# Sparse feed-forward with features on the partitions, for pairs of blocks of rows

## The chip, the cores and the metric

The kernel runs on one core of a Trainium2 chip. The metric is the device time of one execution in microseconds (us), taken as the median over runs. The whole kernel is a chain of eight layers (four pairs of attention and feed-forward); the change touches one of them, the second.

## The reference, cut to what matters

The state `x` has 16 blocks of 128 rows with 256 features. The stage that is changed computes `x = x + ffn(layernorm(x))`, all in float32, with weights 256x1024, 256x1024 and 1024x256:

```
def _sparsify_2to4(h):
    g = h.reshape(B, S, I // 4, 4)
    a = jnp.abs(g)
    _, idx = jax.lax.top_k(a, 2)
    pos = jnp.arange(4)
    mask = (pos == idx[..., 0:1]) | (pos == idx[..., 1:2])
    return (g * mask.astype(g.dtype)).reshape(B, S, I)
h = silu(einsum('bsh,hi->bsi', x, w_gate)) * einsum('bsh,hi->bsi', x, w_up)
h_sparse = _sparsify_2to4(h)
return einsum('bsi,ih->bsh', h_sparse, w_down)
```

Of every four neighbouring features of the 1024, the two of larger size are kept and the others set to zero.

## The kernel before

`sparse_ffn` works on one block `t` (128 rows) at a time. Rows lie on the partitions. `norm_row` (ScalarE) normalises a block into `xn`; `turn_row` (TensorE) transposes its two 128x128 halves into the bank `row_t`; `move_row` (ScalarE) copies them to `xt`. `gate_up` multiplies with `xt` as the stationary operand and 512 columns of weights as the moving one, for two halves `n` of the 1024 features: the rows stay on the partitions of the banks `gate[n]` and `up[n]`, and the features run along them. A float32 matmul of the program stands in the trace as two matmul instructions, each with a weight load of its own; a transpose is one.

Then, for each half: `silu` (ScalarE) reads `gate`, `multiply` (VectorE) forms `h` from it and `up`, `sizes` (ScalarE) takes the absolute value. `sparsify` (VectorE) compares the four features of each group pairwise. As the four are neighbours in a row, every operand of these comparisons and of the four products that write `kept` steps over four elements, 16 bytes. The comparisons give 0 or 1 in 16-bit numbers (`near`, `far`, `ends`, `mids`), which are added and compared with a count.

`turn_down` then transposes `kept` in eight 128x128 pieces into the banks `turned`, ScalarE copies them to `ht` in two pieces (`move`), and eight matmuls of the program with 256 moving columns, over the eight pieces, sum up `down`. `update` (VectorE) adds that to `x` and takes the statistics of the next norm.

The order of each engine is written by hand, with semaphores between engines. TensorE: `gate_up(t)`, `turn_row(t + 1)`, `turn_down(t - 1)`. VectorE: `multiply(t)`, `sparsify(t)`, `update(t - 1)`. Blocks 1 to 14 run in a hardware loop (`Fori`) on each of the three engines; blocks 0 and 15 are written out. At the end `turn_ahead` transposes the first rows of the next stage. The weights were loaded during the stage before. GpSimd only takes two roots, and no transfer but instructions runs beside the stage.

Of the kernel before, what the change touches and what calls it, by code (L numbers as in the profile page):

```python
# [5 lines left out]
BF16 = mybir.dt.bfloat16  # L6
# [3 lines left out]
ALU = mybir.AluOpType  # L10
# [4 lines left out]
P = 128  # L15
# [598 lines left out]
def sparse_ffn(nc, mem, norm, norm_next):  # L614

    I = 1024
    N2 = I // 2
    Q = I // 4
    ctx = Stage(nc)
    with ctx:  # L620
# [6 lines left out]
        def signal(what, per=1, credit=0):  # L627
            return Signal(ctx, nc, f"sf_{what}", per, credit)

        w = mem.sf  # L630
        xt = sb("xt", [P, HC, P])
        act_g = sb("act_g", [P, I])
        h, size = sb("h", [P, I]), sb("size", [P, I])
        kept = sb("kept", [P, I])

        near = sb("near", [P, 2, Q], BF16)
        far = sb("far", [P, 2, Q], BF16)
        ends, mids = sb("ends", [P, Q], BF16), sb("mids", [P, Q], BF16)
        outer, inner = sb("outer", [P, 2, Q], BF16), sb("inner", [P, 2, Q], BF16)
        outer_n, inner_n = sb("outer_n", [P, 2, Q], BF16), sb("inner_n", [P, 2, Q], BF16)  # L640
# [4 lines left out]
        down, row_t = bank("down"), bank("row_t")  # L645
        xn, ahead = sb("xn", [P, H]), sb("ahead", [P, GROUP, H])
        row_normed, row_turned, row_moved = signal("row_normed"), signal("row_turned"), signal("row_moved")
        ahead_normed, ahead_turned, ahead_moved = signal("ahead_normed"), signal("ahead_turned"), signal("ahead_moved")
        gated = signal("gated", 2, 1)
        silued = signal("silued", 2, 2)  # L650
        multiplied = signal("multiplied", 2, 2)
        sized = signal("sized", 2)
        compared = signal("compared", 4)
        counted = signal("counted", 5)
        sparse = signal("sparse", 1, 1)
        turn = signal("turn", 2, 2)
        moved = signal("moved", 2, 2)
        downed = signal("downed", 1, 1)
        added = signal("added", 1, 1)
        stat = signal("stat")  # L660

        with nc.Block() as block:
# [6 lines left out]
            def _(pe):  # L669
                for s, n in ((gated, 1), (turn, 2), (downed, 1)):  # L670
                    pe.sem_inc(s.sem, n)
                pe.wait_ge(mem.sf_loaded.sem, 16 * mem.sf_loads)

                def turn_row(t):
                    pe.wait_ge(row_normed.sem, row_normed.at(t))
                    for c in range(HC):
                        last = pe.transpose(row_t[:, c * P:(c + 1) * P], xn[:, c * P:(c + 1) * P], mem.ident[:, :])
                    last.then_inc(row_turned.sem, 1)
# [8 lines left out]
                def gate_up(t):  # L687
                    pe.wait_ge(row_moved.sem, row_moved.at(t))
                    for n in range(2):
                        pe.wait_ge(silued.sem, silued.at(t, n - 2))  # L690
                        pe.wait_ge(multiplied.sem, multiplied.at(t, n - 2))
                        for out, weight in ((gate, w.wg), (up, w.wu)):
                            for c in range(HC):
                                last = pe.matmul(out[n][:, :], xt[:, c, :], weight[:, c, n * N2:(n + 1) * N2], start=(c == 0), stop=(c == HC - 1))
                        last.then_inc(gated.sem, 1)

                def turn_down(t):
                    pe.wait_ge(sparse.sem, sparse.at(t))
                    for n in range(2):
                        pe.wait_ge(moved.sem, moved.at(t, n - 2))  # L700
                        for k in range(4):
                            c = 4 * n + k
                            last = pe.transpose(turned[n][:, k * P:(k + 1) * P], kept[:, c * P:(c + 1) * P], mem.ident[:, :])
                        last.then_inc(turn.sem, 1)
                    pe.wait_ge(added.sem, added.at(t, -1))
                    for n in range(2):
                        pe.wait_ge(moved.sem, moved.at(t, n))
                        for c in range(4 * n, 4 * n + 4):
                            last = pe.matmul(down[:, 0:H], ht[:, c, :], w.wd[:, c, :], start=(c == 0), stop=(c == I // P - 1))
                    last.then_inc(downed.sem, 1)  # L710

                turn_row(0)
                gate_up(0)
                turn_row(1)
                with pe.Fori(1, B - 1) as t:
                    gate_up(t)
                    turn_row(t + 1)
                    turn_down(t - 1)
                gate_up(B - 1)
                turn_down(B - 2)  # L720
                turn_ahead(0, row_t)
                pe.wait_ge(silued.sem, silued.at(B - 1, 0))
                turn_ahead(1, gate[0])
                turn_down(B - 1)

            @block.scalar
            def _(act):
                act.sem_inc(silued.sem, 2)
                act.sem_inc(moved.sem, 2)

                def silu(t, n):
                    act.wait_ge(gated.sem, gated.at(t, n))
                    act.wait_ge(multiplied.sem, multiplied.at(t, n - 2))
                    act.activation(act_g[:, n * N2:(n + 1) * N2], gate[n][:, :], ACT.Silu).then_inc(silued.sem, 1)

                def sizes(t, n):
                    act.wait_ge(multiplied.sem, multiplied.at(t, n))
                    if n == 0:
                        act.wait_ge(sparse.sem, sparse.at(t, -1))
                    act.activation(size[:, n * N2:(n + 1) * N2], h[:, n * N2:(n + 1) * N2], ACT.Abs).then_inc(sized.sem, 1)  # L740

                def move(t):
                    act.wait_ge(downed.sem, downed.at(t, -1))
                    for n in range(2):
                        act.wait_ge(turn.sem, turn.at(t, n))
                        act.activation(ht[:, 4 * n:4 * n + 4, :].rearrange("p c s -> p (c s)"), turned[n][:, :], ACT.Copy).then_inc(moved.sem, 1)

                def norm_row(t):
                    if not isinstance(t, int) or t >= 1:
                        act.wait_ge(row_turned.sem, row_turned.at(t - 1))  # L750
                    act.activation(xn[:, :], mem.x_tile(t), ACT.Identity, bias=norm.shift[:, bass.ds(t, 1)],
                                   scale=norm.rstd[:, bass.ds(t, 1)]).then_inc(row_normed.sem, 1)

                def move_row(t):
                    act.wait_ge(row_turned.sem, row_turned.at(t))
                    act.activation(xt[:, :, :].rearrange("p c s -> p (c s)"), row_t[:, 0:H], ACT.Copy).then_inc(row_moved.sem, 1)
# [12 lines left out]
                norm_row(0)  # L769
                move_row(0)  # L770
                norm_row(1)
                silu(0, 0)
                sizes(0, 0)
                silu(0, 1)
                sizes(0, 1)
                move_row(1)
                act.wait_ge(norm.shifted.sem, norm.shifted.at(GROUPS - 1))
                with act.Fori(1, B - 1) as t:
                    norm_row(t + 1)
                    silu(t, 0)  # L780
                    sizes(t, 0)
                    silu(t, 1)
                    move(t - 1)
                    sizes(t, 1)
                    move_row(t + 1)
                silu(B - 1, 0)
                sizes(B - 1, 0)
                silu(B - 1, 1)
                move(B - 2)
                sizes(B - 1, 1)  # L790
                for t in range(GROUP):
                    norm_ahead(t)
                move_ahead(0, row_t)
                move_ahead(1, gate[0])
                move(B - 1)

            @block.vector
            def _(dve):
                dve.sem_inc(multiplied.sem, 2)
                dve.sem_inc(sparse.sem, 1)  # L800
                dve.sem_inc(added.sem, 1)
                groups = size[:, :].rearrange("p (q u v) -> p v u q", u=2, v=2)
                fours = size[:, :].rearrange("p (q f) -> p f q", f=4)
                h4, kept4 = (x[:, :].rearrange("p (q f) -> p f q", f=4) for x in (h, kept))

                def multiply(t):
                    dve.wait_ge(sparse.sem, sparse.at(t, -1))
                    for n in range(2):
                        dve.wait_ge(silued.sem, silued.at(t, n))
                        dve.tensor_tensor(h[:, n * N2:(n + 1) * N2], act_g[:, n * N2:(n + 1) * N2], up[n][:, :], ALU.mult).then_inc(multiplied.sem, 1)  # L810

                def sparsify(t):
                    dve.wait_ge(sized.sem, sized.at(t, 1))
                    dve.tensor_tensor(near[:, :, :], groups[:, 0], groups[:, 1], ALU.is_ge).then_inc(compared.sem, 1)
                    dve.tensor_tensor(far[:, 0, :], fours[:, 1], fours[:, 3], ALU.is_ge)
# [3275 lines left out]
```

## Time and profile before

| | |
|---|---|
| time, median of 3 runs | 2070.43 us (2069.07 to 2079.79) |
| profiled execution | span 2074.5 us; its own time is not given beside the span |
| granted TensorE clock, mean over the span | 0.960 of full speed |
| this stage, first gate matmul to last statistics | 491.7 to 693.7 us |
| TensorE busy, 530 to 650 us | 117.51 of 120 us |
| VectorE busy, same stretch | 89.69 of 120 us |
| ScalarE busy, same stretch | 41.86 of 120 us |

Starts are in us from the span's start. In the timeline several instructions of one kind are merged into a row with their count; the time beside it runs from the first one's start to the last one's end. PE is the matmul side of TensorE and PEld its weight loads, which run beside the matmuls; DVE is VectorE, ACT ScalarE, POOL GpSimd. The ends of matmuls are modelled, so their spacing is read from starts.

### The profile page before, as it was taken

What the parts mean: (1) busy time and instruction counts of PE and PEld (TensorE: products, weight loads), DVE (VectorE), ACT (ScalarE), POOL (GpSimd) and SP (SyncE); (2) the same over time, 40 slices, a digit from 0 to 9 for tenths busy, and PEclk for the clock granted to TensorE, in tenths of its full rate; (3) what the DMA queues carried; (4) which work ended last, traced back from release to release, by engine and by line L of the source; (5) the groups of instructions that cost most, each with busy time, mean ns of one, the idle gap of its engine ahead of it and who ended that gap; (6) DMA issues with size and microseconds to landing.
All of it is one profiled execution on the core that took longest, in us unless ns stands there. A gap on an engine that the chain in (4) does not pass through costs nothing. (4 is left out here: it accounts for less than half of the span.)

```text
span 2074.5 us, 42486 instructions
## 1 busy us (share of the span) xinstructions
PE 1853.4 (89%) x12207; PEld 1251.6 (60%) x12216; DVE 1266.8 (61%) x4137; ACT 1026.9 (50%) x2698; POOL 730.7 (35%) x707
## 2 busy tenths in 40 slices
PE   7999999998999888878999989969978799999755
PEld 4677777775565566545666766735545557777533
DVE  6666666665777344656343334368979545656698
ACT  5555555553333443312444434348879524444586
POOL 3333333331000202566455555533300106676410
PEclk9999999999999898979999999989999898999998
DMA  8990000000000000253777776510010111211100
GB/s 305 283 274 1 0 0 0 0 1 0 0 0 0 1 1 33 76 197 120 170 162 169 169 155 136 92 59 2 2 64 1 64 43 26 42 39 36 43 18 24
DMA packets 145607, 145.55 MB, mean 70 GB/s; under 512 B 49376, under 2 KB 133568, under 8 KB 145344
## 3 DMA queue, kind: packets, MB, share of 16 engines
q1 hardware_dynamic: 122432, 113.81, 19.5%
q0 software_dynamic: 23040, 30.01, 8.2%
q8 instruction: 75, 1.23, 0.2%
q14 instruction: 60, 0.49, 0.1%
HBM read 137.12 MB, written 66.44 MB: 98 GB/s over the span
## 5 line engine op out<-in xcount | busy, mean ns | idle before, releaser
L1709 POOL DMA_INDIRECT expert_sums<-moe_rows_in,moe_to x128 | 198.2, 1549 | 158.7 <-DMA expert_sums<-moe_rows_in,moe_to 91.9
L1782 PE MATMUL moe_gate<-moe_places,moe_xt 128*128 x512 | 175.3, 465 | 3.4 <-issue 1.9
L3329 DVE CUSTOM_DVE_ANT_0 ctxt<-wa_score,early 128x128 f32<-128x128 f32 x512 | 114.2, 286 | 101.3 <-PE wa_score L3179 101.3
L1975 DVE COPY moe_ht_e<-moe_turned 128x256 f32<-128x256 f32 x128 | 54.4, 425 | 193.9 <-PE moe_turned L1790 192.5
L570 ACT ACTIVATE ga_prob<-ga_score,ga_neg_max 128x128 f32<-128x128 f32 x256 | 99.6, 390 | 125.7 <-DVE ga_neg_max L443 125.7
L3141 POOL TENSOR_TENSOR ctxt<-ctxt,wa_top 128x512 f32<-128x512 f32 x128 | 131.6, 1040 | 75.4 <-DVE wa_top L3329 75.4
L2065 POOL TENSOR_TENSOR ln_rstd<-ln_var,half 128x4 f32<-128x4 f32 (+1 forms) x16 | 21.5, 1346 | 362.1 <-DVE ln_var L2061 362.1
L190 POOL TENSOR_TENSOR ga_q_inv<-ga_q_sum,half 128x4 f32<-128x4 f32 x64 | 64.4, 1007 | 224.3 <-DVE ga_q_sum L426 224.3
L3278 ACT ACTIVATE wa_pt<-wa_turned 128x512 f32<-128x512 f32 x128 | 76.5, 598 | 129.7 <-PE wa_turned L3188 129.7
L325 PE MATMUL ga_summed<-ga_wo,ga_out_t 128*128 128x256 f32 x512 | 121.2, 380 | 0.7 <-ACT ga_out_t L578 0.7
L1782 PEld LDWEIGHTS moe_gate<-moe_places,moe_xt 128*128 128x128 f32 x512 | 90.5, 189 | 47.2 <-issue 12.1
L249 PE MATMUL ga_proj<-early,ga_xt 128*128 128x512 f32 x252 | 118.6, 593 | 0.0
L1116 POOL DMA_INDIRECT slot_x<-early x96 | 97.8, 1019 | 56.4 <-issue 27.4
L439 DVE SCALAR_TENSOR_TENSOR ga_score<-ga_scored,ga_q_inv,ga_mask 128x128 f32<-128x128 f32 x256 | 72.2, 344 | 51.6 <-PE ga_scored L297 50.1
L325 PEld LDWEIGHTS ga_summed<-ga_wo,ga_out_t 128*128 128x128 f32 x512 | 92.3, 190 | 11.0 <-ACT ga_out_t L578 1.1
L1889 ACT ACTIVATE moe_act_e<-moe_gate 128x176 f32<-128x176 f32 x128 | 40.6, 317 | 100.0 <-PE moe_gate L1782 99.3
L3179 PE MATMUL wa_score<-wa_keys,wa_qd 32*128 32x128 f32 x1024 | 78.9, 294 | 11.6 <-DVE wa_top L3329 9.0
L3188 PE MATMUL wa_turned<-ident,ctxt 128*128 128x128 f32 x512 | 84.3, 290 | 0.0
L3179 PEld LDWEIGHTS wa_score<-wa_keys,wa_qd 32*128 32x128 f32 x1024 | 66.6, 197 | 26.6 <-issue 23.2
L431 DVE COPY ga_qt<-ga_turned 128x512 f32<-128x512 f32 x63 | 43.5, 690 | 62.5 <-PE ga_turned L289 62.4
L297 PEld LDWEIGHTS ga_scored<-ga_kt,ga_qt 128*128 128x128 f32 x512 | 63.3, 191 | 23.6 <-DVE ga_qt L431 13.9
L556 ACT ACTIVATE ga_square<-ga_q_tok 128x128 f32<-128x128 f32 x256 | 75.0, 294 | 1.3 <-DVE ga_q_tok L394 1.3
(491 smaller groups left out, 4777.6 us busy)
## 6 DMA issues: line engine op xcount, KB each, us to landing
moe_places<-in_L_ffn_packed SPq DMA_DIRECT2D x128, 608.0 KB
slot_x<-zeros SPq DMA_DIRECT2D x24, 1076.0 KB, 16.3
moe_rows_in<-slot_x SPq DMA_DIRECT2D x128, 134.5 KB, 3.0
wa_v<-v_ctx SPq DMA_DIRECT2D x16, 180.0 KB, 3.1
early<-in_L_xattn_Wq SPq DMA_DIRECT2D x5, 512.0 KB, 7.8
x<-in_x SPq DMA_DIRECT2D x4, 512.0 KB, 9.6
ga_wo<-in_L_xattn_Wo SPq DMA_DIRECT2D x1, 2048.0 KB, 15.1
expert_sums<-zeros SPq DMA_DIRECT2D x2, 1024.0 KB, 8.4
```

The lines of the kernel that those rows point to most:

```text
L249: last = pe.matmul(proj[m % 2][:, :], lhs[:, c, :], weight[:, c, :], start=(c == 0), stop=(c == HC - 1))
L325: last = pe.matmul(summed[:, 0:H], out_t[:, h, :], w.wo[:, h, :], start=(h == 0), stop=(h == NH - 1))
L556: last = act.activation(square[:, h, :], q_tok[:, n % 2, h * D:(h + 1) * D], ACT.Square, accum_out=q_sum[:, n % 2, h:h + 1])
L570: last = act.activation(prob[:, n % 2, part], score[:, n % 2, part], ACT.Exp, bias=neg_max[:, n % 2, h:h + 1], accum_out=total[:, n % 2, h ...
L1116: pool.indirect_dma_start(out=self.mem.slot_x, out_offset=bass.IndirectOffsetOnAxis(ap=self.slot_to[:, t, k:k + 1], axis=0), in_=self.mem. ...
L1709: pool.indirect_dma_start(out=mem.sums[j % SUMS], out_offset=bass.IndirectOffsetOnAxis(ap=to[:, j:j + 1], axis=0), in_=y[:, j, :], in_offs ...
L1782: last = pe.matmul(both[j % 2][:, 0:2 * FE], xt[:, j % 2, c, :], packed[:, place, c * 2 * FE:(c + 1) * 2 * FE].rearrange("p a n -> p (a n) ...
L3141: pool.tensor_tensor(unit, unit, top[:, k % LOWS, :].unsqueeze(2).to_broadcast([P, QUAD, P]), ALU.subtract).then_inc(lowered.sem, 1)
L3179: last = pe.matmul(score[(QUAD * u + r) % 3][:, x * P:(x + 1) * P], w.qd[rows, j % 2, QUAD * u + x, :], w.keys[rows, j % 2, QUAD * u + x, ...
L3188: last = pe.transpose(turned[k % 2][:, x * P:(x + 1) * P], low[:, k % LOWS, x, :], mem.ident[:, :])
L3278: act.activation(pt[:, (k // 2) % 2, :, k % 2, :], turned[k % 2][:, :].rearrange("p (x m) -> p x m", x=QUAD), ACT.Exp).then_inc(pt_moved.s ...
L3329: ins = dve.tensor_tensor_reduce(unit[:, x, :], score[k % 3][:, x * P:(x + 1) * P], w.table[:, k, x, :], 1.0, NEVER, ALU.add, ALU.max, top ...
```

## The change

The stage is computed with features on the partitions, for a pair `p` of blocks (256 rows) at a time. The columns of the gate and up weights are reordered on the host (and the rows of the down weights with them), so that the four features of a group lie in four different 128-column slices, at the same place in each. There are two sets `s` of four slices. `gate_up(p, u)` takes two slices (a unit `u`, four to a pair): the weights' 128x128 pieces are now the stationary operand, and the 256 normalised rows the moving one. `h`, `size` and `kept` are laid out as slice by row, so each comparison and each product of `sparsify(p, s)` reads and writes whole runs of 256 elements. One of the comparisons is now one instruction of 512 in place of two of 256.

`kept` then has features on the partitions already. `go_down(p, s)` uses it as the stationary operand directly: the transposes into `turned`, the copies to `ht` and the banks for them are gone. `down` has two banks, one for each block of the pair; `xt` and `kept` have two buffers.

The order is new, and there is no hardware loop: all eight pairs are written out on every engine.

```
 def host_layout(inputs):
+    for name in ("L0_ffn_w_gate", "L0_ffn_w_up"):
+        a[name] = np.ascontiguousarray(a[name].reshape(H, 2, P, 4).transpose(0, 1, 3, 2).reshape(H, 1024))
+    a["L0_ffn_w_down"] = np.ascontiguousarray(a["L0_ffn_w_down"].reshape(2, P, 4, H).transpose(0, 2, 1, 3).reshape(1024, H))
...
-        xt = sb("xt", [P, HC, P])
-        h, size = sb("h", [P, I]), sb("size", [P, I])
-        kept = sb("kept", [P, I])
-        ht = sb("ht", [P, I // P, P])
-        turned = [bank(f"turned{j}") for j in range(2)]
+        xt = sb("xt", [P, 2, HC, N])
+        act_g = sb("act_g", [P, 2, 2, N])
+        h, size = sb("h", [P, SETS, V, N]), sb("size", [P, SETS, V, N])
+        kept = sb("kept", [P, 2, SETS * V, N])
+        down, row_t = [bank(f"down{j}") for j in range(2)], bank("row_t")
...
             def _(pe):
+                def turn_rows(p):
+                    pe.wait_ge(row_normed.sem, row_normed.at(2 * p + 1))
+                    behind(pe, row_moved, p - 1)
+                    for c in range(HC):
+                        for i in range(2):
+                            last = pe.transpose(row_t[:, (2 * c + i) * P:(2 * c + i + 1) * P], xn[:, i, c * P:(c + 1) * P], mem.ident[:, :])
...
+                def gate_up(p, u):
+                    n = p * UNITS + u
+                    if u == 0:
+                        pe.wait_ge(row_moved.sem, row_moved.at(p))
+                    behind(pe, multiplied, n - 2)
+                    for out, weight in ((gate, w.wg), (up, w.wu)):
+                        for v in range(2):
+                            f = 2 * u + v
                             for c in range(HC):
-                                last = pe.matmul(out[n][:, :], xt[:, c, :], weight[:, c, n * N2:(n + 1) * N2], start=(c == 0), stop=(c == HC - 1))
+                                last = pe.matmul(out[n % 2][:, v * N:(v + 1) * N], weight[:, c, f * P:(f + 1) * P], xt[:, p % 2, c, :], start=(c == 0), stop=(c == HC - 1))
+                    last.then_inc(gated.sem, 1)
+
+                def go_down(p, s):
+                    pe.wait_ge(sparse.sem, sparse.at(SETS * p + s))
+                    for i in range(2):
+                        if s == 0:
+                            behind(pe, added, 2 * (p - 1) + i)
+                        for f in range(V * s, V * (s + 1)):
+                            last = pe.matmul(down[i][:, 0:H], kept[:, p % 2, f, i * P:(i + 1) * P], w.wd[:, f, :], start=(f == 0), stop=(f == V * SETS - 1))
+                        if s == SETS - 1:
+                            last.then_inc(downed.sem, 1)
...
+                turn_rows(0)
+                for p in range(PAIRS):
+                    gate_up(p, 0)
+                    gate_up(p, 1)
+                    if p >= 1:
+                        go_down(p - 1, 0)
+                        go_down(p - 1, 1)
+                    if p + 1 < PAIRS:
+                        turn_rows(p + 1)
+                    gate_up(p, 2)
+                    gate_up(p, 3)
                 turn_ahead(0, row_t)
+                go_down(PAIRS - 1, 0)
+                pe.wait_ge(silued.sem, silued.at(PAIRS * UNITS - 2))
                 turn_ahead(1, gate[0])
+                go_down(PAIRS - 1, 1)
...
             def _(act):
+                norm_rows(0)
+                move_rows(0)
+                for p in range(PAIRS):
+                    silu(p, 0)
+                    sizes(p, 0)
+                    if p + 1 < PAIRS:
...
+                        norm_rows(p + 1)
+                    silu(p, 1)
+                    sizes(p, 1)
...
+                    silu(p, 2)
+                    sizes(p, 2)
+                    if p + 1 < PAIRS:
+                        move_rows(p + 1)
+                    silu(p, 3)
+                    sizes(p, 3)
...
             def _(dve):
+                def sparsify(p, s):
+                    q = SETS * p + s
+                    of, value = size[:, s, :, :], h[:, s, :, :]
+                    every = size[:, s, :, :].rearrange("p (u v) n -> p v u n", v=2)
+                    out = kept[:, p % 2, V * s:V * (s + 1), :]
+                    dve.wait_ge(sized.sem, sized.at(p * UNITS + 2 * s + 1))
+                    dve.tensor_tensor(near[:, :, :], every[:, 0], every[:, 1], ALU.is_ge).then_inc(compared.sem, 1)
+                    dve.tensor_tensor(far[:, :, :], of[:, 0:2], of[:, 2:4], ALU.is_ge).then_inc(compared.sem, 1)
+                    dve.tensor_tensor(ends[:, :], of[:, 0], of[:, 3], ALU.is_ge).then_inc(compared.sem, 1)
+                    dve.tensor_tensor(mids[:, :], of[:, 1], of[:, 2], ALU.is_ge).then_inc(compared.sem, 1)
...
+                    dve.tensor_tensor(outer[:, :, :], near[:, :, :], far[:, :, :], ALU.add).then_inc(counted.sem, 1)
                     for k in range(2):
+                        dve.tensor_tensor(inner[:, k, :], far[:, 1 - k, :], near[:, k, :], ALU.subtract).then_inc(counted.sem, 1)
...
+                    dve.scalar_tensor_tensor(out[:, 0], outer_n[:, 0, :], 2.0, value[:, 0], ALU.is_ge, ALU.mult)
...
+                for p in range(PAIRS):
+                    multiply(p, 0)
+                    if p == PAIRS - 1:
+                        dve.wait_ge(stat.sem, stat.at(B - GROUP - 1))
+                        norm_next.variance(dve, 0, B - GROUP)
+                    multiply(p, 1)
+                    if p == PAIRS - 1:
+                        norm_next.shifts(dve, 0, 0, B - GROUP)
+                    sparsify(p, 0)
+                    if p >= 1:
+                        update(2 * p - 2)
+                        update(2 * p - 1)
+                    multiply(p, 2)
+                    multiply(p, 3)
+                    sparsify(p, 1)
                 update(B - 2)
                 update(B - 1)
```

On ScalarE `silu(p, u)` and `multiply(p, u)` handle 512 elements as before, `norm_rows(p)` two blocks, and `move_rows(p)` one copy of 512.

## Rows read from the trace of the kernel before

**Rows 1.** Head of the page: span, busy time and instructions by engine.
```profile
span 2074.5 us, 42486 instructions
PE 1853.4 (89%) x12207; PEld 1251.6 (60%) x12216; DVE 1266.8 (61%) x4137; ACT 1026.9 (50%) x2698; POOL 730.7 (35%) x707
```

**Rows 2.** Windows: PE, PEld, DVE, ACT, POOL busy, granted clock, DMA share, GB/s.
```profile
1450.00:1500.00 50.00, 50.00 (x450) 28.94 (x442) 45.54 (x107) 42.31 (x108) 19.34 (x21) 1.00 0.01 2
530.00:650.00 120.00, 117.51 (x423) 71.83 (x422) 89.69 (x182) 41.86 (x80) 0.00 (x0) 1.00 0.00 0
```

**Rows 3.** Waits, 491.5 to 692 us: who for whom, total us, times, longest.
```profile
ACT sf_act_g L734 <- PE sf_up L694: 94.0, 30, 6.0
...
DVE sf_near L814 <- ACT sf_size L740: 14.8, 16, 1.0
...
PE sf_down L709 <- ACT sf_ht L746: 4.3, 15, 0.6
```

**Rows 4.** Timeline of one turn of the loop: start, us, engine, line.
```profile
602.60 0.60 ACT L734 ACTIVATE sf_act_g<-sf_gate 128x512 f32<-128x512 f32 x1 [5.55 <-PE sf_up L694]
...
605.87 0.91 PEld L703 LDWEIGHTS sf_turned<-ident,sf_kept 128*128 128x128 f32 x8
...
607.26 3.32 PEld L709 LDWEIGHTS sf_down<-sf_wd,sf_ht 128*128 128x128 f32 x16 [0.49 <-ACT sf_ht L746]
...
608.25 1.10 DVE L814 TENSOR_TENSOR sf_near<-sf_size 128x512 bf16<-128x512 f32 x1 [0.97 <-ACT sf_size L740]
608.37 0.61 ACT L751 ACTIVATE sf_xn<-x,ln_shift,ln_rstd 128x256 f32 x1
609.25 0.62 DVE L815 TENSOR_TENSOR sf_far<-sf_size 128x256 bf16<-128x256 f32 x1
609.78 0.62 DVE L816 TENSOR_TENSOR sf_far<-sf_size 128x256 bf16<-128x256 f32 x1
...
610.61 0.41 PEld L694 LDWEIGHTS sf_gate<-sf_wg,sf_xt 128*128 128x128 f32 x2
...
611.25 0.19 PEld L694 LDWEIGHTS sf_gate<-sf_wg,sf_xt 128*128 128x128 f32 x1 [0.24 <-issue]
...
611.68 0.19 PEld L694 LDWEIGHTS sf_gate<-sf_wg,sf_xt 128*128 128x128 f32 x1 [0.24 <-issue]
...
614.38 0.66 DVE L839 SCALAR_TENSOR_TENSOR sf_kept<-sf_outer_n,sf_h 128x256 f32<-128x256 bf16 x1
...
614.53 0.60 ACT L734 ACTIVATE sf_act_g<-sf_gate 128x512 f32<-128x512 f32 x1 [5.56 <-PE sf_up L694]
...
614.91 0.45 DVE L844 TENSOR_TENSOR x<-x,sf_down 128x256 f32 x1
...
616.00 0.69 DVE L810 TENSOR_TENSOR sf_h<-sf_act_g,sf_up 128x512 f32<-128x512 f32 x1
```

**Rows 5.** Groups by form, whole span: count, busy us, mean ns, idle before.
```profile
L420 DVE TENSOR_TENSOR ga_k_rms<-ga_k_tok,ga_k_inv 128x512 f32<-128x512 f32 x16 | 11.1, 692 | 7.9 <-POOL ga_k_inv L185 7.9
...
L823 DVE TENSOR_TENSOR sf_outer<-sf_near,sf_far 128x256 bf16<-128x256 bf16 x32 | 7.9, 294 | 0.0
...
L826 DVE TENSOR_TENSOR sf_inner_n<-sf_inner,sf_mids 128x512 bf16<-128x512 bf16 x16 | 6.8, 427 | 0.0
...
L1474 DVE TENSOR_TENSOR la_mixed_t<-la_wide,la_z_inv 128x256 f32<-128x256 f32 x16 | 6.8, 425 | 1.5
...
L1098 DVE SCALAR_TENSOR_TENSOR early<-early 128x128 f32<-128x128 f32 x3 | 0.9, 291 | 0.1
```

**Rows 6.** Timeline of the stage's start: the first matmuls after a pause.
```profile
491.70 3.68 PE L694 MATMUL sf_gate<-sf_wg,sf_xt 128*128 128x512 f32 x4 [0.47 <-ACT sf_xt L756]
```

**Rows 7.** Timeline of the stage's end: last transposes, last matmuls, last statistics.
```profile
686.51 1.97 PE L703 MATMUL sf_turned<-ident,sf_kept 128*128 128x128 f32 x8 [3.13 <-DVE sf_kept L839]
...
688.46 4.35 PE L709 MATMUL sf_down<-sf_wd,sf_ht 128*128 128x256 f32 x16
...
693.30 0.43 DVE L846 BATCH_NORM_STATS2 stats<-x 128x6 f32<-128x256 f32 x1
```

More of the change, by code:

```diff
@@ L642, in sparse_ffn @@
+        near, far = sb("near", [P, 2, N], BF16), sb("far", [P, 2, N], BF16)
+        ends, mids = sb("ends", [P, N], BF16), sb("mids", [P, N], BF16)
+        outer, inner = sb("outer", [P, 2, N], BF16), sb("inner", [P, 2, N], BF16)
+        outer_n, inner_n = sb("outer_n", [P, 2, N], BF16), sb("inner_n", [P, 2, N], BF16)
         gate = [bank(f"gate{j}") for j in range(2)]
         up = [bank(f"up{j}") for j in range(2)]
-        turned = [bank(f"turned{j}") for j in range(2)]
-        down, row_t = bank("down"), bank("row_t")
@@ L662, in sparse_ffn, with behind @@
+        downed, added, stat = signal("downed"), signal("added"), signal("stat")
+        def behind(engine, sig, n):
+            if n >= 0:
+                engine.wait_ge(sig.sem, sig.at(n))
         with nc.Block() as block:
@@ L697, in turn_down @@
[L697 to L710, printed above, removed]
@@ L736, in sizes @@
[L736 to L746, printed above, removed]
@@ L748, in norm_row, with silu @@
[L748 to L756, printed above, removed]
+                def silu(p, u):
+                    n = p * UNITS + u
+                    act.wait_ge(gated.sem, gated.at(n))
+                    behind(act, multiplied, n - 2)
+                    act.activation(act_g[:, n % 2, :, :].rearrange("p v n -> p (v n)"), gate[n % 2][:, :], ACT.Silu).then_inc(silued.sem, 1)
@@ new lines, in sizes, with norm_rows @@
+                def sizes(p, u):
+                    s, k = divmod(u, 2)
+                    act.wait_ge(multiplied.sem, multiplied.at(p * UNITS + u))
+                    if k == 0:
+                        behind(act, sparse, SETS * (p - 1) + s)
+                    act.activation(size[:, s, 2 * k:2 * k + 2, :], h[:, s, 2 * k:2 * k + 2, :], ACT.Abs).then_inc(sized.sem, 1)
+                def norm_rows(p):
+                    behind(act, row_turned, p - 1)
+                    for i in range(2):
+                        t = 2 * p + i
+                        act.activation(xn[:, i, :], mem.x[:, t, :], ACT.Identity, bias=norm.shift[:, t:t + 1],
+                                       scale=norm.rstd[:, t:t + 1]).then_inc(row_normed.sem, 1)
@@ L758, in norm_ahead, with move_rows @@
+                def move_rows(p):
+                    act.wait_ge(row_turned.sem, row_turned.at(p))
+                    if p >= 2:
+                        act.wait_ge(gated.sem, gated.at((p - 2) * UNITS + UNITS - 1))
+                    act.activation(xt[:, p % 2, :, :].rearrange("p c n -> p (c n)"), row_t[:, :], ACT.Copy).then_inc(row_moved.sem, 1)
                 def norm_ahead(t):
@@ L768, in _ @@
                 act.wait_ge(norm.shifted.sem, norm.shifted.at(GROUPS - 2))
[L769 to L792, printed above, removed]
+                norm_rows(0)
[4 more added lines that the diff above has]
+                    if p + 1 < PAIRS:
+                        if 2 * (p + 1) == B - GROUP:
+                            act.wait_ge(norm.shifted.sem, norm.shifted.at(GROUPS - 1))
+                        norm_rows(p + 1)
+                    silu(p, 1)
+                    sizes(p, 1)
+                    if p == PAIRS - 1:
+                        for t in range(GROUP):
+                            norm_ahead(t)
+                    silu(p, 2)
[4 more added lines that the diff above has]
+                    sizes(p, 3)
```

132 lines of the change are left out of this document (34 added, 98 removed).

## The prediction

> **What bounds the kernel now.** I read the page's head first: TensorE is busy 89% of a span of 2074.5 us [rows 1], so a stage is bound by it unless its own rows say otherwise. Then the windows of this stage: from 530 to 650 us TensorE is busy 117.51 of 120 us at a granted clock of 1.00 (2.4 GHz), VectorE 89.69 and ScalarE 41.86 [rows 2]. The waits say the same from the other side: ScalarE's first `silu` of a block waits for the up matmuls, 94.0 us in all, while TensorE waits only 4.3 us in 15 waits, for the copies to `ht` [rows 3]. So TensorE's own work sets the pace, with one short stall in each block.
>
> The timeline gives the period: `silu` starts at 602.60 and again at 614.53, so a block takes 11.93 us and a pair 23.86 [rows 4]. Inside it, wide gate loads follow each other every 0.43 us (611.25, 611.68): that is the pace of 512 moving columns. Sixteen make 6.86 us. The eight transposes of `kept` take 0.91 us, so 0.114 each, and the two row transposes 0.23. Then 0.49 us of stall for `ht`, and 16 down matmuls of 256 columns from 607.26 to the next gate load at 610.61, 3.35 us or 0.209 each. These sum to 11.84 of the 11.93; the loop's edge shows no gap of its own.
>
> **The change on TensorE.** A unit is 16 matmul instructions of 256 columns. Half of 0.43 is 0.215, and the down matmuls show 0.209 for the same form (128x128 stationary, 256 moving, float32); I take 0.213. A pair then has 64 in `gate_up` (13.63 us, a unit being 3.41), 32 in `go_down` (6.82) and 4 row transposes (0.46): 20.9 us against 23.86. The columns streamed are the same; what goes is two times 0.91 of transposes and 0.49 of stall with the small gaps beside it. With 0.209 and 0.215 a pair is 20.5 or 21.1, so the gain is 2.8 to 3.4 us a pair; I take 3.0.
>
> **Whether the narrow matmuls hide their loads.** A load takes 0.19 us [rows 4] and now stands before every 0.213 us of gate and up streaming, in place of every 0.43. In the down matmuls of before it does too, and they still come every 0.209: the load is hidden, with only 0.02 us to spare. The Trainium skill (TensorE: Matmul & The Clock Gate, under "The mechanism") says otherwise: a weight load overlaps with matmuls in flight only if it goes to other row groups, and all these loads fill all rows. By that rule, with the rows' durations, a pair of before would take 38.6 us and one of after 39.7, some 9 us slower in all. The trace does not agree, since a pair of before takes 23.86.
>
> **VectorE.** The set of `sparsify` has the same elements as a block had, 1024 a partition, so there is one set for each block as before. From `near` at 608.25 to the end of the last `kept` at 615.04 it takes 6.8 us [rows 4]. Instructions overlap by some 0.09 us (`far` lasts 0.62, the next starts 0.53 on). No row shows a contiguous compare; the bounds are the strided price (512 in 1.10, 256 in 0.62 to 0.66) and contiguous float32 rows of the same kind: 512 in 0.692 and 256 in 0.425 [rows 5]. I take the contiguous end, since 0.692 has both inputs in SBUF as here and differs from `near` only in its stride. For the products that write `kept`, an instruction with a scalar over 128 columns takes 0.291, so 0.42 for 256. Start to start: `near` and `far` 0.60 each, `ends` and `mids` 0.335 each, `outer` 0.335 (0.427 for 512 in 16 bit), `inner` twice 0.20 (0.294), the two sums 0.335 each, `kept` four times 0.335. That is 4.6, and 4.7 to the end of the last: 2.1 less than 6.8.
>
> **Does that leave TensorE the bound?** The new order makes a ring between VectorE and ScalarE, since `multiply(p, 2)` stands behind both updates and a set, and `silu(p, 1)` behind `sizes(p, 0)` and `norm_rows`. From the end of one pair's second set: multiply 0.69, sizes 0.63, two norms 1.0 (0.61 each less the overlap), silu 0.60, multiply 0.69, sizes 0.63, the first set 4.7, two updates 2.2 (614.91 to 616.00 is one), multiply 0.69, sizes 0.63, `move_rows` 0.60, silu 0.60, multiply 0.69, sizes 0.63, the second set 4.7: 19.7 us. Twelve handovers add 0.6 at 0.05 each, an estimate (at nothing the ring is 19.4, at 0.12 each it draws level with TensorE), and ScalarE's overlaps give back 0.3. So 20.0 us against TensorE's 20.9: TensorE stays the bound by 0.9 us a pair. The ring binds once a set takes more than 5.15 us, and each 0.1 us beyond costs 0.2 a pair. `go_down(p-1, 1)` needs a set that ends about 7 us into the pair and comes at 10.2; `move_rows` ends about 0.9 us before the next pair's first matmul. What ScalarE loses (the copies to `ht`) was beside the path and counts only as that stall. GpSimd and the queues carry no new work.
>
> **Start and end.** Before, the first gate matmul starts at 491.70 and four of them take 3.68 us [rows 6], a pace of about 0.85, the lower level of the clock (1.2 GHz). This costs 1.7 us over some 3.4, and will again. The first pair must norm two blocks (0.5 more), turn four pieces (0.2) and copy 512 instead of 256 (0.2): start at 492.6. In pair 0 the second half's inputs come late: unit 0 ends at 497.7; silu, multiply, sizes, two norms, silu, multiply and sizes follow by 503.0, the set ends at 507.7, `multiply(0, 2)`, sizes and `move_rows(1)` at 509.7, while unit 3 ends at 508.4: a stall of 1.4 once. Then TensorE: 492.6 + 32 units 109.1 + 1.7 + seven times 6.82 (47.7) + seven times 0.46 (3.2) + 1.4 = 655.7. The last set needs silu, multiply and sizes (2.3 with handovers) and 4.7: 662.7. Here TensorE has stood idle and pays the low clock again, as before (686.51: eight transposes in 1.97, sixteen matmuls in 4.35 [rows 7]). `go_down(7, 1)` has 16 matmuls: 3.4 + 1.6 + 0.3 = 5.3 us, then add and statistics 1.1: 669.1. Before, the stage ends at 693.73 [rows 7]. The sum is -24.6 us; I take -24. Against the profiled span that is 2050.5. The profiled span lies 4 us above the median, and the same difference against the median of 2070.43 gives 2046.4.
>
> **Written out.** The three engines lose their loops. That brings more code, at about 4.8 matmuls a us. In stretches that are written out TensorE issued 450 in 50 us, 9 a us, and was busy all of it [rows 2], so I cost it at nothing; if code came late it would show as gaps at each pair.
>
> **Rivals.**
> 1. *The ring binds a little* (0.08). The `kept` products keep their strided pace, 0.54 start to start, for their mix of 16- and 32-bit operands. A set is 5.5, the ring 21.6, 0.7 above TensorE in seven pairs, and 1.6 more at the end: 24 less 6.5 gives 17.5, so 2053. For it: no row has that mix contiguous. Against: the whole strided price is explained by the step.
> 2. *The price does not depend on the step* (0.06). Sets stay 6.8; the ring is 24.2 against 23.86 now, so 2 us more over seven pairs, less a little for the shorter tail: 2072, no change. For it: both operands read SBUF. Against: 0.692 against 1.10 for 512.
> 3. *The loads show* (0.04), the other side. If the gate and up loads are not hidden, 64 times 0.19 is 12.2 us a pair, 97 in all, less 24: 2143. The gain of 3.0 us a pair is gone from 0.047 us exposed for each of 64. For it: only 0.02 us of room. Against: the down matmuls' own pace.
> 4. *Anything unnamed* (0.02), about no change, late code or a semaphore chain that I missed.
>
> **How the numbers follow.** The forecast has 0.80. A measurement of this kernel can tell about 0.5%, 10.4 us. Forecast and rival 1 lie beyond it: faster 0.88. Rivals 2 and 4 give 0.08 of same, rival 3 0.04 of slower. The gain a pair of 2.8 to 3.4 gives 22 to 28 us; with the set's bounds 17 us at the low end, and the spread of the runs themselves, the range is 2038 to 2058. It leaves out rivals 2 to 4, and a tenth of the rest.
>
> **What the profile would show.** No rows for `turned` and `ht`. Gate and up matmuls of 256 columns every 0.21 us. `near` and `far` at 0.69 for 512, `ends`, `mids` and `kept` at 0.42. Pairs of 20.9 us, TensorE hardly waiting; the stage's last statistics at 669 or so. The forecast is wrong if TensorE waits for `row_moved` (then the ring binds), or if narrow matmuls come slower than every 0.22 us.

## The result, and the profile after

The changed kernel takes 2047.37 us in the median (2043.93 to 2050.54, 4 runs) against 2069.75 (2068.96 to 2079.79, 4 runs) for the kernel before: a ratio of 0.9885 with a 95% interval of [0.9862, 0.9908], so 19 to 29 us less. Timed again on another chip beside later experiments (6 runs against 11), it gave 0.9878 [0.9839, 0.9917]. The forecast was 2046.4, in a range of 2038 to 2058.

First the window that answers to [rows 2]. TensorE now has no idle time in it at all, and VectorE's busy time fell from 89.69 to 76.81 us.

```profile
530.00:650.00 120.00, 120.00 (x568) 105.65 (x567) 76.81 (x195) 36.45 (x64) 2.27 (x1) 1.00 0.00 1
```

The waits of the changed kernel from 491.5 to 668 us, answering to [rows 3] (who for whom: total us, times, longest):

```profile
ACT sf_act_g L729 <- PE sf_up L693: 70.7, 24, 7.3
...
DVE sf_near L801 <- ACT sf_size L736: 10.4, 15, 0.7
...
PE sf_down L702 <- DVE sf_kept L826: 2.5, 1, 2.5
...
PE sf_gate L693 <- ACT sf_xt L749: 2.1, 2, 1.4
```

TensorE's waits are one at the end, for the last set (2.5 us), and those at the start for `xt`, of which 1.4 is the stall in pair 0. None is left in the pairs between; before, there were 15, about one in every block.

The timeline of one pair, weight loads alone, answering to [rows 4]:

```profile
567.41 0.57 PEld L674 LDWEIGHTS sf_row_t<-ident,sf_xn 128*128 128x128 f32 x4
...
571.30 1.70 PEld L693 LDWEIGHTS sf_gate<-sf_xt,sf_wg 128*128 128x128 f32 x8
573.03 1.70 PEld L693 LDWEIGHTS sf_up<-sf_xt,sf_wu 128*128 128x128 f32 x8
574.76 1.70 PEld L693 LDWEIGHTS sf_gate<-sf_xt,sf_wg 128*128 128x128 f32 x8
...
581.66 6.88 PEld L702 LDWEIGHTS sf_down<-sf_wd,sf_kept 128*128 128x128 f32 x32
588.57 0.58 PEld L674 LDWEIGHTS sf_row_t<-ident,sf_xn 128*128 128x128 f32 x4
```

A unit goes from 571.30 to 574.76, 3.46 us, 0.216 a matmul. The down matmuls take 6.91, and the pair, from one turn of the rows to the next, 21.16 us: 2.7 less than the 23.86 of two blocks before. The groups of VectorE, answering to [rows 5] and to the strided rows of [rows 4]:

```profile
L801 DVE TENSOR_TENSOR sf_near<-sf_size 128x512 bf16<-128x512 f32 x16 | 11.1, 692 | 10.4 <-ACT sf_size L736 10.4
L802 DVE TENSOR_TENSOR sf_far<-sf_size 128x512 bf16<-128x512 f32 x16 | 10.9, 684 | 0.0
...
L803 DVE TENSOR_TENSOR sf_ends<-sf_size 128x256 bf16<-128x256 f32 x16 | 6.7, 419 | 0.0
...
L819 DVE SCALAR_TENSOR_TENSOR sf_kept<-sf_outer_n,sf_h 128x256 f32<-128x256 bf16 x16 | 6.7, 417 | 0.1
```

Start and end of the stage, answering to [rows 6] and [rows 7]:

```profile
493.79 3.68 PE L693 MATMUL sf_gate<-sf_xt,sf_wg 128*128 128x256 f32 x8 [0.69 <-ACT sf_xt L749]
...
511.39 1.99 PE L693 MATMUL sf_gate<-sf_xt,sf_wg 128*128 128x256 f32 x8 [1.39 <-ACT sf_xt L749]
```

```profile
666.15 3.72 PE L702 MATMUL sf_down<-sf_wd,sf_kept 128*128 128x256 f32 x16 [2.49 <-DVE sf_kept L826]
...
670.37 0.43 DVE L833 BATCH_NORM_STATS2 stats<-x 128x6 f32<-128x256 f32 x1
```

From the first row norm (491.24, before 490.08) to the last statistics' end (670.80, before 693.73) the stage takes 179.6 us, before 203.6: 24.1 less. The profiled span fell by 32.0, from 2074.5 to 2042.5. The first attention stage was 1.2 longer here, so 9 us fell after this stage, where no code changed, 7.7 of them between the start of the next stage and the first matmuls of the experts, some 280 us later. There the granted clock of the one profile and of the other differ. Before:

```profile
694.40:720.00 25.60, 22.94 (x100) 13.23 (x104) 2.07 (x9) 11.60 (x17) 7.57 (x16) 0.81 0.01 2
...
800.00:830.00 30.00, 28.10 (x240) 22.86 (x237) 13.01 (x39) 11.71 (x23) 14.18 (x15) 0.83 0.16 56
```

After, in the corresponding stretches:

```profile
671.50:697.00 25.50, 22.70 (x136) 13.35 (x136) 4.47 (x12) 12.76 (x20) 8.28 (x17) 1.00 0.01 2
...
777.00:807.00 30.00, 29.11 (x280) 21.91 (x280) 18.51 (x48) 12.94 (x26) 18.18 (x19) 1.00 0.20 70
```

This goes with the clock, not with the change. The stretch takes 275.6 us in this profile, at a mean granted clock of 0.94, and 279.7 in the second profile of the same kernel, at 0.91. The kernel before has 283.3 at 0.90; but its old order written out (below) has 278.5 at 0.93, and the changed order with strided compares (below) 283.0 at 0.90. So the stage is best read by its own pairs, and the medians of many runs for the rest.

### The profile page after: what moved, and what is told of

It is laid out like the page before. It is cut to its first block and busy times, and to the rows that moved or that the text cites. A ratio compares the mean times of both kernels' runs of the same rounds, so it can differ in the third digit from the quotient of the medians.

```text
span 2042.5 us, 42221 instructions
## 1 busy us (share of the span) xinstructions
PE 1822.0 (89%) x12335; PEld 1277.1 (63%) x12344; DVE 1233.2 (60%) x4121; ACT 1011.1 (50%) x2658; POOL 732.3 (36%) x707
```

## The experiments

**Is it the loops?** The kernel before with its loops written out:

```
-                with pe.Fori(1, B - 1) as t:
+                for t in range(1, B - 1):
```

and the same on ScalarE and VectorE.

> The kernel before with its three hardware loops written out, nothing else. Theory T (TensorE's own work sets the pace, the loops cost nothing): the stage from the first row norm to the last statistics stays at 203.6 us within 1 us, a block at 11.93 us, the time within 0.3%. Rival W (part of the gain comes from writing out): the stage falls by 5 us or more.

Ratio to before 0.9992 [0.9966, 1.0018]. In the timeline of ScalarE `move_row` comes every 12.05 us, where before it was 11.93:

```profile
587.43 0.39 ACT L756 ACTIVATE sf_xt<-sf_row_t 128x256 f32<-128x256 f32 x1
...
599.48 0.38 ACT L756 ACTIVATE sf_xt<-sf_row_t 128x256 f32<-128x256 f32 x1
```

Writing out gives nothing; it costs 0.12 us a block. The rows show where: from the first transpose of `kept` to the first down matmul TensorE takes 1.44 us (585.24 to 586.68), before 1.28 (605.98 to 607.26), and its waits for `ht` sum to 6.4 us against 4.3. Why the copies to `ht` come later is open. The stage was 208.1 us, 4.5 more than before, outside what theory T allowed: 1.7 from the blocks, the rest at start and end, where the clock was lower. The granted clock was 0.81 from 488 to 515 us (0.94 in before's profile), and the last sixteen down matmuls took 5.25 us (before 4.35).

**Is it VectorE's contiguous operands?** The kernel before with only its columns reordered:

```
-                groups = size[:, :].rearrange("p (q u v) -> p v u q", u=2, v=2)
-                fours = size[:, :].rearrange("p (q f) -> p f q", f=4)
+                groups = size[:, :].rearrange("p (u v q) -> p v u q", u=2, v=2)
+                fours = size[:, :].rearrange("p (f q) -> p f q", f=4)
...
+    for name in ("L0_ffn_w_gate", "L0_ffn_w_up"):
+        a[name] = np.ascontiguousarray(a[name].reshape(H, 256, 4).transpose(0, 2, 1).reshape(H, 1024))
+    a["L0_ffn_w_down"] = np.ascontiguousarray(a["L0_ffn_w_down"].reshape(256, 4, H).transpose(1, 0, 2).reshape(1024, H))
```

`h4` and `kept4` are regrouped in the same way.

> The kernel before, rows still on the partitions, but with gate and up columns reordered so that the four features of a group lie 256 apart, and all operands of the sparsify set are contiguous. Both theories expect near at 0.69 and kept at 0.42 us, a set shorter by 2.1 us. Theory T: a block stays at 11.93 us, only the last set at the stage's end counts, the stage falls by about 2 us, the time by 2. Rival V (the gain comes from VectorE's cheaper set): the stage falls by 10 us or more, towards the 24 of the change.

Ratio 0.9986 [0.9961, 1.0011]. Its groups, and two copies of the rows in ScalarE's timeline:

```profile
L814 DVE TENSOR_TENSOR sf_near<-sf_size 128x512 bf16<-128x512 f32 x16 | 11.1, 693 | 15.0 <-ACT sf_size L740 15.0
...
L837 DVE SCALAR_TENSOR_TENSOR sf_kept<-sf_outer_n,sf_h 128x256 f32<-128x256 bf16 x16 | 6.7, 419 | 0.0
```

```profile
595.98 0.39 ACT L756 ACTIVATE sf_xt<-sf_row_t 128x256 f32<-128x256 f32 x1
...
607.91 0.39 ACT L756 ACTIVATE sf_xt<-sf_row_t 128x256 f32<-128x256 f32 x1
```

The set is as cheap as in the changed kernel, and the block is still 11.93 us. The stage fell by 3.4 us to 200.2, all at its ends, against 2 expected. The last set is 1.95 us shorter (4.79 for 6.74). Another 1.1 us lies behind it and is the clock's: before's profile has the low level there (transposes 1.97 us, down matmuls 4.35 [rows 7]), this one the high level (1.09 and 3.69). As TensorE sets the pace, VectorE's 2 us a block bought nothing but the tail.

**Does the changed order need the contiguous operands?** The changed kernel, with `size` stored so that the compares are strided again:

```
-        h, size = sb("h", [P, SETS, V, N]), sb("size", [P, SETS, V, N])
+        h, size = sb("h", [P, SETS, V, N]), sb("size", [P, SETS, N, V])
...
-                    act.activation(size[:, s, 2 * k:2 * k + 2, :], h[:, s, 2 * k:2 * k + 2, :], ACT.Abs).then_inc(sized.sem, 1)
+                    act.activation(size[:, s, :, 2 * k:2 * k + 2].rearrange("p n v -> p v n"), h[:, s, 2 * k:2 * k + 2, :], ACT.Abs).then_inc(sized.sem, 1)
```

> The changed kernel with size stored with the four features innermost, so that the four compares are strided again while the rest stays contiguous. A set grows by 1.25 us (near 0.4, far 0.4, ends and mids 0.2 each). Ring theory: the ring of about 20.0 us grows by 2.5 to 22.5 and passes TensorE's 21.2; 1.3 us a pair in seven pairs and 1.3 at the end, 10 to 11 us slower; if the strided writes also lengthen the absolute values on ScalarE beyond 0.63 us, each 0.1 us of that adds 0.4 a pair. Rival (TensorE has ample room, no ring): only the 1.3 us at the end.

Ratio 0.9948 [0.9918, 0.9977] to before, so more than half of the gain is gone. A pair takes 22.9 us, and TensorE waits for `xt`:

```profile
PE sf_gate L693 <- ACT sf_xt L749: 11.9, 7, 3.3
```

```profile
L736 ACT ACTIVATE sf_size<-sf_h 128x512 f32<-128x512 f32 x32 | 36.0, 1124 | 65.4 <-DVE sf_h L793 65.4
L801 DVE TENSOR_TENSOR sf_near<-sf_size 128x512 bf16<-128x512 f32 x16 | 17.4, 1088 | 18.1 <-ACT sf_size L736 18.1
```

The compares are at their strided price, and ScalarE's strided write too (1.124 us, 0.630 contiguous). The stage takes 197.4 us, 17.8 more than the changed kernel's 179.6. The expectation gives 10 to 11, and some 14 more for ScalarE's writes at the price measured; it is too high since the ring is narrower than it says, as the padding below shows. So the reordering is not what gains the time, but the new order can't do without it: in each pair VectorE and ScalarE wait for each other in a ring, and a slow set makes it longer than TensorE's work.

**Does TensorE's work set the pace?** The changed kernel with the transposes put back, unread:

```
                     for i in range(2):
+                        for k in range(V):
+                            pe.transpose(turned[:, k * P:(k + 1) * P], kept[:, p % 2, V * s + k, i * P:(i + 1) * P], mem.ident[:, :])
```

> The changed kernel with the eight transposes of kept for each block put back on TensorE, into a bank that nobody reads; no copies, no wait. Theory T: each costs its 0.114 us on the path, 128 of them 14.6 us, a pair goes from 21.2 to 23.0 us. Rival (the ring of VectorE and ScalarE sets the pace of the changed kernel): less than 7 us, since TensorE would have room.

Ratio 0.995 [0.9929, 0.9971]. The row transposes of two pairs in the timeline of the loads:

```profile
595.61 0.58 PEld L674 LDWEIGHTS sf_row_t<-ident,sf_xn 128*128 128x128 f32 x4
...
618.53 0.57 PEld L674 LDWEIGHTS sf_row_t<-ident,sf_xn 128*128 128x128 f32 x4
```

A pair is 22.92 us, 1.76 more: sixteen times 0.110. In the pairs each transpose stands on the path in full. The stage takes 193.6 us, which is 14.0 more: 12.3 in seven pairs, and the rest at start and end, where eight of the last pair's transposes fall into TensorE's wait for the last set (1.6 us of it are left, of 2.5) and the clock at the start is lower (0.87 from 488 to 515 us, against 0.94).

**How wide is the ring?** One and three more compares of 512 elements in each set, results unused:

```
+                    for spare in (outer, inner, outer_n)[:3]:
+                        dve.tensor_tensor(spare[:, :, :], of[:, 0:2], of[:, 2:4], ALU.is_ge).then_inc(compared.sem, 1)
```

with the counts of `compared` raised to suit (`[:1]` in the run with one).

> The changed kernel with one more compare of 512 contiguous elements (0.60 us) in each set, result unused. Ring theory with a ring of 20.0 against TensorE's 21.2: 1.2 us more in a ring is just level, so the stage grows by 0 to 1.5 us, 0.6 of them at the end. If the ring bound already: 1.2 us a pair, 9 us.

> The same with three more compares of 512 in each set (1.8 us). Ring theory: the ring goes to 23.6, 2.4 above TensorE's 21.2, in seven pairs 17 us, and 1.8 at the end: the stage grows by 18 to 19 us. If VectorE's busy time alone counted (about 16 of 21 us a pair now, 19 with this): only the 1.8 us at the end.

With one more a pair stays at 21.16 us (574.16 to 595.32 between two `move_rows`), with three it goes to 22.40:

```profile
579.82 0.58 ACT L749 ACTIVATE sf_xt<-sf_row_t 128x512 f32<-128x512 f32 x1
...
602.22 0.58 ACT L749 ACTIVATE sf_xt<-sf_row_t 128x512 f32<-128x512 f32 x1
```

Three compares add 3.6 us to the ring (0.60 each, two sets), so the ring without them is 18.8 us, not 20.0, and has 2.4 us of room under 21.16. The rows between 578.58 and 600.98 us of this run, where the ring sets the pace, give its parts: the sets without their padding 4.63 us each, the two updates 1.58, all the rest 7.95.

The stages took 183.4 and 194.4 us, 3.8 and 14.8 more. The first is more than expected, the second less. In both the last sixteen down matmuls ran at the low clock (5.41 and 6.09 us, against 3.72 in the changed kernel's profile), which is 1.7 and 2.4 us by chance; and the ring was narrower than I had it. Each of the two was run once: 2050.92 and 2062.84 us, with one run of the kernel before at 2063.83.

**What does a weight load cost?** The changed kernel with gate and up matmuls of 128 and of 64 moving columns (shown for 128; for 64 there are four pieces in place of two):

```
-                            for c in range(HC):
-                                last = pe.matmul(out[n % 2][:, v * N:(v + 1) * N], ..., xt[:, p % 2, c, :], ...)
+                            for i in range(2):
+                                for c in range(HC):
+                                    last = pe.matmul(out[n % 2][:, v * N + i * P:v * N + (i + 1) * P], ..., xt[:, p % 2, c, i * P:(i + 1) * P], ...)
```

> The changed kernel with each gate and up matmul split into two of 128 moving columns, one for each block of the pair: twice the weight loads, the same columns. Streaming 128 columns takes half of 0.216, 0.108 us; a load takes 0.19. If a load is hidden only up to the pace of the matmuls, the pace becomes 0.19 to 0.20 us each and a unit goes from 3.46 to 6.1 to 6.4 us: 2.7 to 2.9 us for each of 32 units, 86 to 93 us slower. If loads never show (they would come ahead at the pace of the transposes, 0.114): a unit at 3.6, 5 us slower in all. If loads do not overlap at all: 0.30 each, 9.5 a unit, over 190 us.

> The changed kernel with each gate and up matmul split into four of 64 moving columns, so four times the weight loads. In the run with 128 columns a load and a matmul came every 0.112 us although a load is shown as 0.19 us long, so the shown length is not what a load occupies. Theory L (a load occupies about 0.11 us): the pace stays at 0.11 us each, a unit goes from 3.46 to 7.1 us, a pair from 21.2 to 35.8, the stage 115 us longer. Theory C (only columns count): 0.056 us each, a unit at 3.6 us, the stage 5 us longer.

Loads in the timeline, at 128 columns (sixteen to a row) and then at 64 (thirty-two):

```profile
571.70 1.87 PEld L694 LDWEIGHTS sf_gate<-sf_xt,sf_wg 128*128 128x128 f32 x16
573.48 1.87 PEld L694 LDWEIGHTS sf_up<-sf_xt,sf_wu 128*128 128x128 f32 x16
```

```profile
603.10 3.65 PEld L694 LDWEIGHTS sf_up<-sf_xt,sf_wu 128*128 128x128 f32 x32
606.67 3.65 PEld L694 LDWEIGHTS sf_gate<-sf_xt,sf_wg 128*128 128x128 f32 x32
```

With 128 columns 16 loads take 1.79 us, 0.112 each, though each is shown as 0.19 long; a pair is 21.64 us, only 0.48 more, and the time of the one run 2051.63 us. The expectation of 86 to 93 us was wrong by its main branch; its second, that loads never show, gave 5 us, and the stage took 183.0 us, 3.4 more. With 64 columns 32 loads take 3.57 us, again 0.112 each, with half the columns: a unit is 7.15 us and a pair 35.93. So theory L's pace holds at the full clock: a load and its matmul come no faster than every 0.11 us, whatever the columns. At the 256 columns of the change there is 0.10 us of room. Whether it is the load alone that takes 0.11 us, or the two instructions together, these runs do not show.

But the stage took 338.0 us, 158 more, where theory L had 115, and the one run 2206.09 us. The other 43 us are the clock. Here are TensorE's rows of this run, earlier in the stage:

```profile
568.51 7.03 PE L694 MATMUL sf_up<-sf_xt,sf_wu 128*128 128x64 f32 x32
575.33 9.73 PE L703 MATMUL sf_down<-sf_wd,sf_kept 128*128 128x256 f32 x32
...
588.86 3.74 PE L694 MATMUL sf_up<-sf_xt,sf_wu 128*128 128x64 f32 x32
```

From 500 to 575 us the granted clock was 0.50, the lower of the two levels, with TensorE busy all of the time, and 32 matmuls with their loads took 6.83 us, 0.213 each. It rose between 580 and 581 us, within the first pair's down matmuls of 256 columns, and from 590 to 650 us it was 1.00 over the same 64-column work. Why it stayed low so long here is open, and this kernel was run once.

**What is left at start and end?** First `move_rows` ahead of the third silu:

```
+                    if p + 1 < PAIRS:
+                        move_rows(p + 1)
                     silu(p, 2)
                     sizes(p, 2)
-                    if p + 1 < PAIRS:
-                        move_rows(p + 1)
```

> The changed kernel with move_rows(p + 1) ahead of silu(p, 2) on ScalarE instead of behind sizes(p, 2). Theory: the wait of 1.39 us for it in the first pair goes, all other pairs are bound by TensorE's work and stay at 21.2 us: the stage 1.2 to 1.4 us shorter. Rival: move_rows now holds up silu(p, 2), as it waits for the row transposes, and the pair grows.

TensorE's wait for it in pair 0 is gone. One of 0.34 us for VectorE's `multiply` stands in its place, so 1.05 us are gained: from the second gate group of pair 0 to the first of pair 1 it takes 11.30 us (498.77 to 510.07), in the changed kernel's profile 12.35 (499.04 to 511.39). The pairs stay at 21.16 us. Yet the stage took 180.9 us, 1.3 more than the changed kernel's: at its start the low clock cost 0.8 us more, and the last sixteen down matmuls took 5.30 us for 3.72. The one run took 2048.80 us. Then with the end reordered too, so that TensorE has matmuls of the pair before left to do while VectorE makes the last set:

```
+        down_of = lambda p: [up[0], last_down] if p == PAIRS - 1 else down
...
+                go_down(PAIRS - 2, 1)
                 turn_ahead(0, row_t)
...
+                for t in range(B - 4, B):
+                    update(t)
```

> The changed kernel with move_rows early as in the run before, and with the second half of the sixth pair's down matmuls moved behind the last unit, their updates behind the last set, and the last pair's sums in two other banks, so that TensorE works while VectorE makes the last set. Theory (only start and end have room left): from the last unit's end TensorE has 6.9 us of its own work, the last set is ready about when that ends, 3.5 us of matmuls and 1.1 of update follow: about 11.5 us from the last unit's end to the stage's end, but that unit ends 3.45 us earlier, 3 to 4 us in all, and 1.4 at the start: the stage 4 to 5 us shorter where the clock levels are the same, 0.2% of the time. Rival: the new waits at the end (for the bank up[0], for the updates) cost it back, 0 to 1 us.

> The changed kernel unchanged, timed beside the others on one chip. Theory: ratio to before within 0.9885 plus or minus 0.003; the part from the first row norm to the last statistics again 179 to 182 us, pairs at 21.16 us, the difference to its other profile in the clock levels at the stage's start and end.

The matmuls of its end have no wait among them:

```profile
657.80 0.60 PE L682 MATMUL sf_row_t<-ident,sf_ahead 128*128 128x128 f32 x4
658.24 1.89 PE L706 MATMUL sf_up<-sf_wd,sf_kept 128*128 128x256 f32 x8
659.97 1.89 PE L706 MATMUL sf_last_down<-sf_wd,sf_kept 128*128 128x256 f32 x8
661.69 0.60 PE L682 MATMUL sf_gate<-ident,sf_ahead 128*128 128x128 f32 x4
662.13 1.89 PE L706 MATMUL sf_up<-sf_wd,sf_kept 128*128 128x256 f32 x8
663.86 1.89 PE L706 MATMUL sf_last_down<-sf_wd,sf_kept 128*128 128x256 f32 x8
```

From the turn at 657.80 to the stage's end at 666.67 are 8.9 us; in the second profile of the unchanged order 11.6, from 657.71 to 669.34. The stages are 176.7 and 179.6 us: 2.9 less, not 4 to 5. The end gave 2.7 where 3 to 4 were expected, and the start's 1.05 went to the clock again (0.89 from 484 to 515 us against 0.94). The unchanged kernel came out as expected, with pairs of 21.16 us. The medians are 2042.97 and 2046.73, the ratios to before 0.9845 [0.9806, 0.9884] and 0.9878 [0.9839, 0.9917]. It is likely the best version, but these intervals overlap.

## Why the prediction was right

**What bounds the kernel.** Right, and shown twice: contiguous operands alone left the block at 11.93 us, and each transpose put back cost its 0.11 us (0.110; the 0.114 that I read from a row of eight has the same end effect as the 0.209 below).

**TensorE's pair.** Forecast 20.9 us, measured 21.16. The pace of narrow matmuls is 0.216 us, not 0.213. The 0.209 that I took as its lower bound, from 3.35 us over 16 loads, was an end effect: the first load of a group comes ahead of its matmul. Rows of 32 show 6.88 us from the first load's start to the last one's end, so (6.88 - 0.19) / 31 = 0.216. The gain was 2.7 us a pair, just under the 2.8 that I gave as the least.

**The loads.** They are hidden, as forecast, but the argument misread the rows. I took the shown length of 0.19 as what a load occupies and saw 0.02 us of room. The runs with 128 and 64 columns show 0.11, so there was 0.10. The Trainium skill's rule on row groups (TensorE: Matmul & The Clock Gate, "The mechanism") fares worse still: at 128 columns, all rows filled, load and matmul together take 0.112 us, less than the load's own shown length. The Trainium skill says in the same section that a load may also be pulled ahead if it goes to the background weight buffer, and the traces agree with that sentence rather than with the rule that I took.

**VectorE.** The set is 4.71 us, from 577.18 to 581.89, as forecast (4.7); every instruction came at the contiguous price. The ring was put at 20.0 us and measured at 18.8. The mis-sized term is the two updates: I took 2.2 us from a row of the loop, and the run padded by three, where the ring binds, has 1.58. It is the loop that made the row long: one update takes 1.09 us there (614.91 to 616.00), and 0.80 in the old order written out (594.26 to 595.06). The rest is small: 0.15 for the two sets, and 0.4 for ScalarE's steps and the multiplies between them with their handovers (7.95 us for the 8.4 of the sum).

**Start and end.** The stall of 1.4 us in pair 0 came as 1.39. The low clock at the start came too. The 1.6 us for a low clock at the end did not: the last sixteen matmuls took 3.72 us after an idle time of 2.5, the full pace. In the run with the early `move_rows` it did come, with the same order there. So it is a chance of each execution, not a term to be added. It made good what the slower matmuls cost (32 units times 0.05, seven times 0.09 for the down matmuls), and so the sum of 24.6 met 24.1 more closely than its parts deserved. Before's profile did pay, some 1.1 us as the contiguous run shows, so at equal clock the stage gained 23. The median is luck in part, too: it lies 1.0 us from the forecast, and the four runs spread over 6.6; the profiled span was forecast at 2050.5 and came at 2042.5, by the clock of the next stage.

**Written out.** Costed at nothing, and shown: no gain, at most 0.12 us a block the other way in the old form.

**The rivals.** Rivals 1 and 2 fell with the prices of the set. Rival 1's mechanism is real: strided compares, with ScalarE's strided write, close the ring and take more than half of the gain back. Rival 3 is refuted by the pace. Nothing unnamed (rival 4) was found in this stage.

So where the 24.1 us came from: 18.9 from the pairs, of which 12.3 are the transposes of blocks 1 to 14 and 6.6 the stall for `ht` with the small gaps about it; and 4.8 from the shorter tail, from the last up matmul to the last statistics. The tail's parts are the cheaper last set (2.0), its transposes and the copies to `ht` (1.5), and the clock (1.1). Some 0.4 is left for the start. The transposes' part and the set's were tested by themselves; the stall's and the tail's others are read from rows.

## What to carry to other kernels

When an operand is transposed only to become the stationary side of the next matmul, computing it transposed from the start takes the transposes, their copies and the wait away at once; the streamed columns stay the same, and the doubling of weight loads is free here, since a matmul of 256 columns takes 0.216 us and a load with its matmul can come every 0.11. Where the bound is TensorE, cheapening VectorE does nothing by itself, but measure the ring of the other engines by padding it: here it says that 2.4 of 21.2 us are free. And read a stage by its period, since its whole length moved by 1 to 3 us from profile to profile with the clock's level at its ends.

## What the runs showed of the hardware

- A float32 weight load is shown as 0.19 us long, but loads with their matmuls come every 0.112 us at a granted clock of 1.00, with 128 moving columns and with 64. At 0.50 those with 64 columns come every 0.213 us.
- In the run with 64 columns the granted clock stayed at 0.50 from 492 to 580 us, through unbroken work, though TensorE was busy 135.00 of the first window's 135 us. The clock of that window, 0.76, is the mean of the two levels, not a third one. The same work then ran at the full clock:

```profile
515.00:650.00 135.00, 135.00 (x870) 132.48 (x870) 39.81 (x98) 19.13 (x33) 0.00 (x0) 0.76 0.00 1
```

```profile
650.00:690.00 40.00, 40.00 (x312) 38.63 (x312) 16.42 (x40) 7.60 (x13) 0.00 (x0) 1.00 0.01 2
```

- The spread between runs goes with the clock. Of 31 runs of the kernel before on one chip, the two with the highest mean granted clock (0.970) took 2057.64 and 2061.86 us, the two with the lowest (0.953) 2080.71 and 2088.00. That is the size of the whole gain, and why the single profile's 32 us says less than the pairs' 2.7.
- In the hardware loop of the kernel before, VectorE's statistics start 0.60 us after the start of the add that they need (614.91 to 615.51); written out, 0.46 (594.26 to 594.72). It lay off the path in both. Why is open.
- ScalarE's absolute value of 512 float32 elements takes 0.630 us to a contiguous output and 1.124 to one that steps over four elements.
